# Expert attention at the boundary between rows: another order of the X-bank fills and of what reads them

## The reference

```python
sx = einsum('bsh,ndh->bnsd', layernorm(x), hl_w) + hl_b          # per head
q = einsum('bnsd,neod->bneso', sx, wq); k = sx @ wk; v = sx @ wv
att = softmax(einsum('bnesd,bntd->bnest', q, k) * d ** 0.5 + causal)
out = where(sx == 0, 0, einsum('bnest,bntd->bnesd', att, v))     # per head and expert
gs = softmax(out @ gate_w + gate_b)                              # over experts
hn = layernorm(sum_e out_e * gs_e + resid)                       # -> z, zn
hx = layernorm(mlp(hn) + hn)                                     # fc1, relu, fc2, each masked
return hx * softmax(hx @ fgate_w)                                # per head
```

## Time and profile before

| | |
|---|---|
| median of three runs | 2044.35 us |
| the profiled execution | 2043.27 us |
| its span | 2041.3 us |
| expert attention | some 570 to 1420 us of the span |
| busy TensorE, VectorE, ScalarE, GpSimd | 84%, 66%, 38%, 30% of the span |

### The profile page before, as it was taken

One profiled execution on the slowest core, in us unless ns is written; L12 is line 12 of the kernel. 1 busy time (PEld: TensorE's weight loads), 2 busy tenths in 40 slices (PEclk: granted clock), 3 DMA queues, 4 the chain that ended last, 5 costly groups with the idle time before them and its releaser, 6 DMA issues. The chain is left out here.

```text
span 2041.3 us, 45282 instructions
## 1 busy us (share of the span) xinstructions
PE 1713.3 (84%) x15237; PEld 1253.0 (61%) x15240; DVE 1350.3 (66%) x4295; ACT 775.0 (38%) x2210; POOL 602.4 (30%) x906
## 2 busy tenths in 40 slices
PE   1499999999669988888888888872899999788887
PEld 1266666666535555555555555551788888677776
DVE  6276666666526666666666666664766666588887
ACT  2254445454234444444444444420222222343443
POOL 2522222222134333333333333333211112222221
PEclk9999999999789887777777777775555555688988
DMA  2000000000000000000000000000000000000000
GB/s 112 1 2 0 0 0 0 0 0 0 1 1 1 2 1 0 0 0 0 0 0 0 0 0 0 0 1 0 1 0 0 0 0 1 1 5 5 6 4 13
DMA packets 6979, 8.13 MB, mean 4 GB/s; under 512 B 6272, under 2 KB 6272, under 8 KB 6784
## 3 DMA queue, kind: packets, MB, share of 16 engines
q1 hardware_dynamic: 6912, 7.25, 1.0%
HBM read 5.71 MB, written 1.54 MB: 4 GB/s over the span
## 5 line engine op out<-in xcount | busy, mean ns | idle before, releaser
L962 POOL TENSOR_SCALAR_AFFINE_SELECT ex_pT<-ex_pT 128x512 f32<-128x512 f32 (+1 forms) x256 | 135.7, 554 | 315.0 <-ACT ex_pT L1176 272.9
L604 ACT ACTIVATE al_prob<-al_S,al_negmax 94x94 f32<-94x94 f32 (+1 forms) x512 | 146.2, 376 | 180.0 <-DVE al_negmax L731 180.0
L505 PE MATMUL al_S<-al_kpad,al_qT 128*94 128x376 f32 x384 | 166.4, 516 | 0.0
L682 POOL TENSOR_TENSOR al_kpad<-al_kT,al_quad_mask 128x1504 f32<-128x1504 f32 x32 | 86.2, 2694 | 186.2 <-ACTq L619 186.2
L731 DVE TENSOR_REDUCE al_negmax<-al_S 94x2 f32<-94x376 f32 (+1 forms) x192 | 99.2, 542 | 62.6 <-PE al_S L506 56.7
L1599 POOL TENSOR_TENSOR ta_kk<-ta_ext 94x320 f32<-94x320 f32 x64 | 60.4, 962 | 246.2 <-DVE ta_qkn L1779 161.6
L1250 DVE TENSOR_REDUCE ex_negmaxA<-ex_R 128x4 bf16<-128x512 f32 x128 | 89.1, 696 | 56.9 <-PE ex_R L1028 51.4
L971 POOL TENSOR_TENSOR ex_zrstd<-ex_zvar,neg_half 94x16 f32<-94x16 f32 x34 | 98.6, 2900 | 28.9 <-DVE ex_zvar L1329 28.9
L741 DVE RECIPROCAL al_rec<-al_O 128x188 f32<-128x188 f32 x64 | 84.9, 1327 | 32.1 <-PE al_O L543 32.1
L1169 ACT ACTIVATE ex_pT<-ex_T 128x496 f32<-128x496 f32 x128 | 74.8, 584 | 76.0 <-PE ex_T L1066 76.0
L1176 ACT ACTIVATE ex_pT<-ex_T 128x496 f32<-128x496 f32 x128 | 74.8, 584 | 73.8 <-PE ex_T L1045 73.7
(11 more groups left out here) (321 smaller groups left out, 4413.3 us busy)
## 6 DMA issues: line engine op xcount, KB each, us to landing
tok_xin<-x_t SPq DMA_DIRECT2D x4, 760.0 KB, 7.3
wsb<-weights SPq DMA_DIRECT2D x1, 2531.0 KB, 14.0
out<-stream SPq DMA_DIRECT2D x16, 94.0 KB
tok_par<-tok_w SPq DMA_DIRECT2D x1, 4.5 KB, 1.7
```

Of the source, the lines that this page charges most:

```text
L505: nc.tensor.matmul(S[0:P, k, 0:2 * N], q, s, start=True, stop=False)
L604: last = nc.scalar.activation(p[:, k, cols], S[0:P, k, cols], ACT.Exp, bias=negmax[g % 2][:, m:m + 1])
L682: nc.gpsimd.tensor_tensor(kpad[par][:].rearrange("p j g n -> p j (g n)"), kT[:].rearrange("p g n -> p (g n)").unsqueeze(1).broadcast_to([1 ...
L962: nc.gpsimd.affine_select(out=view, in_=view, compare_op=ALU.is_ge, fill=0.0, base=shift, pattern=[[0, NH], [1, cols]], channel_multiplier ...
```

## The change

The order in which the X bank is filled and read around the boundary between turns changes, on all four engines.

- The ring becomes znT, fg, sx, pickA, kb01, kb23, q01, pickB, fc1, k, q23, v, xT, fc2. The xT fill moves from the first quarter of the next turn to the last quarter of the turn that normalises the row (behind max_scores), so xT of row t is made in turn t. In the first quarter znT goes ahead of `queries`, and fg ahead of `max_scores`. pickB goes ahead of `queries` in e = 2, q23 ahead of them in e = 3, and v ahead of max_scores.
- ScalarE copies qm ahead of the exponential of heads 0 and 1. In e = 1 and 3 the copies of kb01 and v stand between the two. tA_used is now signalled by that exponential itself; tA_exp is gone. fexp moves to e = 1, gate_exp and xT to the third slot of e = 3.
- GpSimd does rstd, zrstd and mixing at the head of quarters 1, 2 and 3, ahead of that quarter's causal pair. For zrstd and the mixing this is one pair earlier; rstd keeps its place.
- VectorE's list becomes: z reduces, hx mask | final gate logits (own tile ftop) | z adds | maxima(ru,2), mask(rt,3) | statistics, moments | zmean | pick A | maxima(ru,3), mask(ru,0) | zvar | xn | pick B | maxima(rf,0), mask(ru,1) | gate logits | h1m | zn | maxima(rf,1) | gate weights gs | mask(ru,2) | fout | hx add, which now reads fc2 of the same turn (row rm) at its end.

The diff, mostly its added lines:

```diff
@@ -879,10 +880,10 @@
-        FILLS = [("xT", FRONT), ("znT", MLP), ("fg", LAST), ("sx", FRONT),
+        FILLS = [("znT", MLP), ("fg", LAST), ("sx", FRONT),
...
-                 ("q23", FRONT), ("v", FRONT), ("fc2", MLP)]
+                 ("q23", FRONT), ("v", FRONT), ("xT", LN), ("fc2", MLP)]
...
...
@@ -1053,7 +1054,7 @@
-                    pe.wait_ge(sem["tA_used"], u + 1)
+                    need(pe, sem["tA_used"], u)
...
...
@@ -978,6 +968,17 @@
+                    r = t - UNIT
+                    if valid(r):
+                        p = pT[e % 2]
+                        pool.wait_ge(sem["tB_used"], r * NE + e + 1)
+                        pool.wait_ge(sem["tA_used"], r * NE + e + 1)
+                        pool.sem_inc(sem["settled"], 1)
+                        for first, cols, shift in ((0, K0, 0), (N, K1, QB)):
+                            view = p[:, :, first:first + cols]
+                            nc.gpsimd.affine_select(out=view, in_=view, compare_op=ALU.is_ge, fill=0.0, base=shift,
+                                                    pattern=[[0, NH], [1, cols]], channel_multiplier=-1)\
+                                .then_inc(sem["causal_done"], 1)
...
...
@@ -1097,39 +1098,39 @@
+                    if e == 1 and valid(rt):
+                        pe.wait_ge(sem["o_used"], NE * (rt + 1))
+                        fill(t, "pickA", picks(odd, slice(0, P)))
...
+                    if valid(nr):
+                        queries(nr, npar, ne).then_inc(sem["tA_full"], 1)
+                    if e == 0 and valid(rl):
+                        fill(t, "fg", by_halves(P, NH, lambda h: znT[odd][:, h * P:(h + 1) * P], lambda h: w("fgate")))
+                    if e == 1 and valid(rf):
+                        pe.wait_ge(sem["sx_used"], 2 * (rf + 1))
+                        fill(t, "kb01", padded_keys((0, 1)))
+                    if e == 3 and valid(rf):
+                        fill(t, "v", [(X[:, 0:C], sxT[odd][:, 0:K0], w("ewv")),
+                                      (X[:, C:2 * C], sxT[odd][:, QB:NP], w("ewv"))])
+
...
+                    if e == 3 and valid(t):
+                        pe.wait_ge(sem["xn_ready"], t + 1)
+                        fill(t, "xT", by_halves(C, P, lambda h: xn[:, h, :], lambda h: ident[0:P, 0:P]))
...
...
@@ -1167,32 +1168,32 @@
+                    if e == 1 and valid(rl):
+                        act.wait_ge(sem["fgate_ready"], rl + 1)
+                        nc.scalar.activation(fexp[:], fgate[:], ACT.Exp).then_inc(sem["fexp_ready"], 1)
+                    if e == 3 and valid(rf):
+                        act.wait_ge(sem["q23_full"], rf + 1)
+                        used("q23_used", qTb[odd][:, 2:4, 0:N], ALL, slice(0, 2 * N))
+
+                    if valid(nr):
+                        act.wait_ge(sem["tA_full"], nr * NE + ne + 1)
+                        nc.scalar.activation(qm[ne % 2][:], T[:, 0, QCOL:QCOL + N], ACT.Copy).then_inc(sem["m_used"], 1)
...
+                        act.wait_ge(sem["v_full"], rf + 1)
+                        for s, rows in enumerate((ALL, slice(QB, 128))):
+                            nc.scalar.activation(vals[odd][rows, s, :, 0:D],
+                                                 X[rows, s * C:(s + 1) * C].rearrange("p (n d) -> p n d", n=NH), ACT.Copy)\
+                                .then_inc(sem["v_used"], 1)
+                    if valid(ru):
+                        if not valid(nr):
+                            act.wait_ge(sem["tA_full"], u + 2)
+                        nc.scalar.activation(pT[e % 2][:, 0:2, :], T[:, 0:2, 0:PAIR], ACT.Exp).then_inc(sem["tA_used"], 1)
...
...
@@ -1200,12 +1201,12 @@
+                    if e == 3 and valid(rt):
+                        act.wait_ge(sem["gate_ready"], rt + 1)
+                        nc.scalar.activation(gate_exp[:], gate[:], ACT.Exp).then_inc(sem["gexp_ready"], 1)
+                    if e == 3 and valid(t):
+                        act.wait_ge(sem["xT_full"], t + 1)
+                        used("xT_used", xT[:], slice(0, C), slice(0, N))
...
...
@@ -1218,12 +1219,6 @@
...
@@ -1273,10 +1268,6 @@
...
@@ -1284,6 +1275,14 @@
+                if valid(rl):
+                    dve.wait_ge(sem["fg_full"], rl + 1)
+                    gates = X[0:P, 0:HALVES * NH].rearrange("p (h n) -> p h n", h=HALVES)
+                    link(red(ftop[:], gates, AX.X, ALU.max))
+                    tt(fgate[:], gates, ftop[:].unsqueeze(2).broadcast_to([P, HALVES, NH]), ALU.subtract)\
+                        .then_inc(sem["fgate_ready"], 1)
+                    dve.wait_ge(sem["fgate_ready"], rl + 1)
+                    dve.sem_inc(sem["fg_used"], 1)
...
...
@@ -1294,14 +1293,6 @@
...
@@ -1313,13 +1304,13 @@
+                if valid(rt):
+                    pick_heads(rt, 0, "pickA")
...
...
@@ -1328,8 +1319,20 @@
+                if valid(t):
+                    dve.wait_ge(sem["rstd_ready"], t + 1)
+                    need(dve, sem["xT_full"], t)
+                    for h in range(HALVES):
+                        last = ts(xn[:, h, :], stream[:, t * HALVES + h, :], moments[:, h, 0:1], rstd[:, h:h + 1],
+                                  ALU.subtract, ALU.mult)
+                    last.then_inc(sem["xn_ready"], 1)
...
+                if valid(rf):
+                    maxima(rf, 0)
+                if valid(ru):
+                    mask_values(ru, 1, par)
+                if valid(rt):
...
...
@@ -1338,21 +1341,10 @@
...
@@ -1360,6 +1352,17 @@
+                if valid(rf):
+                    maxima(rf, 1)
+                if valid(rt):
+                    dve.wait_ge(sem["gexp_ready"], rt + 1)
+                    flat = gate_exp[:].rearrange("p h n e -> p (h n) e")
+                    link(red(top[:], flat, AX.X, ALU.add))
+                    link(nc.vector.reciprocal(top[:], top[:]))
+                    tt(gate[:].rearrange("p h n e -> p (h n) e"), flat,
+                       top[:].unsqueeze(2).broadcast_to([P, HALVES * NH, NE]), ALU.mult).then_inc(sem["gs_ready"], 1)
+                if valid(ru):
+                    mask_values(ru, 2, par)
...
...
@@ -1368,17 +1371,10 @@
+                if valid(rm):
+                    dve.wait_ge(sem["fc2_full"], rm + 1)
+                    tt(hx[:], X[0:P, 0:HALVES * C].rearrange("p (h c) -> p h c", h=HALVES), over_halves("fc2_b"), ALU.add)\
+                        .then_inc(sem["fc2_used"], 1)
...
```

More of the change, by code:

```diff
@@ L831, in expert_attention @@
         top = sb("top", [P, HALVES * NH])
+        ftop = sb("ftop", [P, HALVES])
         gate_exp = sb("gate_exp", [P, HALVES, NH, NE])
@@ L953, in body @@
                 for e in range(NE):
[L954 to L964, removed]
                     r = t - LN
-                    if e == 0 and valid(r):
+                    if e == 1 and valid(r):
                         rstds(r)
@@ L1099, in body @@
                         scores(ru, par, e, (2, 3)).then_inc(sem["tB_full"], 1)
[L1100 to L1108, removed]
                     if e == 0 and valid2(rm):
@@ L1112, in body @@
                                                  lambda h: ident[0:P, 0:P]))
-                    if e == 1 and valid(rf):
-                        pe.wait_ge(sem["sx_used"], 2 * (rf + 1))
-                        fill(t, "kb01", padded_keys((0, 1)))
+                    if e == 1 and valid(rt):
+                        pe.wait_ge(sem["o_used"], NE * (rt + 1))
+                        fill(t, "pickA", picks(odd, slice(0, P)))
                     if e == 2 and valid(rt):
@@ L1119, in body @@
                         fill(t, "q23", projections((2, 3)))
+                    if valid(nr):
[8 more added lines that the diff above has]
+                                      (X[:, C:2 * C], sxT[odd][:, QB:NP], w("ewv"))])
                     if valid(fr):
                         max_scores(fr, fpar, fe)
-                    if e == 0 and valid(rl):
-                        fill(t, "fg", by_halves(P, NH, lambda h: znT[odd][:, h * P:(h + 1) * P], lambda h: w("fgate")))
                     if e == 1 and valid(rf):
@@ L1169, in body @@
                         nc.scalar.activation(pT[e % 2][:, 2:4, :], T[:, 2:4, 0:PAIR], ACT.Exp).then_inc(sem["tB_used"], 1)
[L1170 to L1186, removed]
                     if e == 0 and valid2(rm):
@@ L1220, in body @@
                         used("k_used", kT[odd][:, 0:N], ALL, slice(0, N), ACT.Identity, bias=one_row[:], scale=D ** 0.5)
[L1221 to L1226, removed]
             act.wait_ge(sem["consts"], CONSTS)
@@ L1274, in body @@
                 odd = 1 - par
[L1276 to L1279, removed]
                 if valid(rz):
@@ L1296, in body @@
                     mask_values(rt, 3, odd)
[L1297 to L1304, removed]
                 if valid(t):
@@ L1315, in body @@
                     last.then_inc(sem["stats_ready"], 1)
-                if valid(rt):
-                    pick_heads(rt, 0, "pickA")
                 if valid2(rz):
```

(15 more changed lines are left out.)

7 lines of the change are left out of this document (1 added, 6 removed).

## The result

The changed kernel takes 2019.71 us (median of 4 runs, 2016.77 to 2022.82) against 2044.31 us of the kernel before: a ratio of 0.988, 95% interval 0.986 to 0.990, 24.6 us less. The forecast was 1979 us. The time lies in the range (1940 to 2035) and on the side that was named, but the gain is 0.38 of the one forecast. It stands nearest to rival (b), in which the clock falls in every turn: 2029.

The account below looks back on a forecast made before the run. TensorE, nearly always busy, was held by a clock halving at turn boundaries: 22 turns from 25.59 to 22.8 us save 61 us, three earlier turns 4, giving 1979 us; own range 1960 to 2000, 8-in-10 range 1940 to 2035.

Parts of the forecast that it names:

- rival (b): Expert attention: clock falls in every turn as now, but the turn shortens to 24.9 us; total 2029 us; chance 0.17.
- The turn at the high level, 21.5 us: Expert attention: one turn without a clock fall, summed along VectorE and TensorE to 20.95 us, with corrections 21.5.
- A fall was priced at 3.4 us: Per turn: 10.1 us at the low level lose 4.4 us, less the 1.0 us kb01 wait absorbed.
- I take 4 turns in 10: Share of turns in which the clock falls, bounds 0 and 10; gives a mean turn of 22.8 us.
- the three early ones: Three turns ahead of the 22: 24.0 us each falling to 22.8, a gain of 4 us.
- the undecided size: Boundary between rows: about 1 us of TensorE idleness may or may not lower the clock; less should keep it high.
- hx ends 1.72 after scores(0) starts: Turn boundary: mask, fout and hx on VectorE end 1.72 us after scores(0) starts, so TensorE waits 1.0 us.
- the z adds: First quarter, VectorE: adds meeting GpSimd's causal pair every turn cost 0.4 us; by the skill's rule the turn is 22.1.
- kb01 waits 1.0: First pick: zmean stands ahead of pick_heads, so kb01 waits about 1.0 us, where it had 0.18.
- rival (c): Slower: the new kb01 wait prolongs the low stretch to 17 us, turn 27.0 us, total 2075 us; chance 0.15.
- GpSimd covered: GpSimd's new order costs nothing: third causal pair covered by 3 us, the mix ahead of the fourth also covered.
- xn costs nothing: Reading xn a turn ahead costs nothing: rstd is ready some 5 us before, and xn fills idle time before pickB.

Follow-up runs that it names:

- x2: Changed kernel with six extra unused matmuls on TensorE between scores(0) and the znT fill, in the wait for hx: 1968.6 us, ratio 0.965.
- x7: Kernel before with one part of the change alone: VectorE reads the final gate logits ahead of maxima(ru, 2). 2019.7 us, ratio 0.988.
- x10: Kernel before with two VectorE changes alone: final gate logits read ahead of maxima(ru, 2), hx added at the turn's end ahead of fout. 1969.8 us, ratio 0.965.
- x3: Changed kernel with VectorE's gate weights gs moved behind fout, so that GpSimd's mixing starts after fout: 2004.1 us, ratio 0.982.
- x11: x1 with four extra unused matmuls on TensorE ahead of the pickA fill, in the wait for ScalarE's copy of sx: 1909.4 us, ratio 0.935.
- x1: Changed kernel with VectorE's hx add moved ahead of fout: 1944.7 us, ratio 0.952.
- x8: Changed kernel with GpSimd's old order: zrstd and the mixing behind their quarter's causal pair. 2045.0 us, ratio 1.001.
- x9: Changed kernel with the xT fill back in the next turn's first quarter, ahead of znT: 2054.4 us, ratio 1.0055.
- x4: Kernel before with four extra unused matmuls on TensorE between scores(0) and the xT fill, in the wait for hx: 1982.7 us, ratio 0.970.

## Why the prediction was wrong

**What held.** The clock is what the turn turns on; sx no longer waits for the gate logits; VectorE's wait for the mixing is gone. The turn at the high level, 21.5 us, was 21.8 in x2 with its extra matmuls, but in part by luck: there kb01 waits 0.42 us where the sum has 1.0, and pickA 1.09 where it has nothing. A fall was priced at 3.4 us; in x2 a turn with 10.2 us at the low level lasts 25.7, 3.9 more than one without. The changed kernel itself has no turn without a fall among the 22, so its 24.72 against the 24.9 of rival (b) does not test the price by itself.

**The step that failed: "I take 4 turns in 10".** The clock falls in all of them, 22 of 22. With 1.0 in place of 0.4 the same sum gives 24.9 us a turn, 15 us less over 22 turns and 3 more over the three early ones: 2032, against 2019.7 measured. So this term is the miss of 41 us and more. Of the 12 us left, 4 are the turn (24.72) and 5 the early turns, which lasted 69.9 us where they had lasted 72.1; 3 are not placed, and the start of the block varies by more.

Three things are in the term. I called about 1 us the undecided size from one wait of 1.07 us that was survived; x7, with 0.93 in each turn, has a low stretch in every one, and that single row was the exception. The wait is not 1.0 but 1.74 us. And I read only every other fall. The level in the earlier trace rows falls at 1014.6, when the wait for hx had just begun: scores end at 1014.55, and the row that waited starts a microsecond later.

```profile
1015.51 0.89 PE L992 MATMUL ex_X<-ident,ex_xn 94*64 94x94 f32 x4 [0.96 <-DVE ex_hx L1278]
```

This wait can't have made the level fall. So it is with 11 of the 22 falls of the kernel before; the other 11 come some 0.65 us after the end of their wait (1.02 us, then 0.50 from 786.0). A size of the boundary wait at which the level is undecided, on which the 0.4 rests, can't be read from these rows. x10's fall without a boundary wait says the same.

**"hx ends 1.72 after scores(0) starts".** In the profiled turn above it is 2.38 (scores start at 993.96, hx ends at 996.34). The rest of the turn has fout with 2.3 us from its first step to hx where I took 1.54: I moved GpSimd's mixing earlier and counted what it freed, but did not look at what VectorE does at its new time. The rule of the Trainium skill (SBUF — State Buffer, "Who interferes with whom") that the prediction applied to the z adds applied here as well. The trace agrees with it: the 8-column product stands until a multiply of GpSimd is through, 0.75 us against 0.16, fout stands beside the causal pair, 0.68 against 0.29, and x3, where neither runs beside them, gives both lengths back.

**"kb01 waits 1.0".** 0.19 in the changed kernel, since TensorE is at the low level there, as the argument against rival (c) had it; 0.42 and 0.61 in x2 and x11, where it is not. Above all pickA, ahead of it, waits 1.1 to 1.4 us in x1 and x2, a wait that my sum did not have: I had followed the X bank's ring, but not the buffer sxT, which the copy of sx must wait for.

**"GpSimd covered", "xn costs nothing".** As costs these were right; what I missed is that the parts carry one another. hx as the last of VectorE's list puts all of its second half on the boundary, so GpSimd's order there is worth 25 us (x8; it moves zrstd and the mixing together, and the trace has the wait at zrstd), and xT ahead of it 35 us (x9). That they pay back what the late hx takes, and no more, is argued from x7, which is as fast without any of them.

**Open.** The difference of 0.87 us a turn is not divided further. TensorE's listed waits hardly changed, 2.5 to 2.3 us a turn, so it lies in the 0.9 us less of low level and in the work that left the low stretch, as argued and not shown. What makes the level fall is open too. That TensorE's waits matter is shown: where hx comes earlier (x1, x10) or matmuls stand in the wait (x2, x4, x11), the low level shrinks. But the idle time does not sort the kernels: over the 22 turns x7 has TensorE idle least of all, 1.94 us a turn, with 11.2 us at the low level, and x2 has 2.45 with 2.0. A rival, that the level follows how much work the matmuls around the boundary are and not how long TensorE stands, fits x2, x4 and x11 as well and was not tried alone; for that one would add the same matmuls where TensorE does not wait. Why a fall follows 0.93 us in x7 and not 1.07 at 735.91 was not tried either.

## What to carry to other kernels

Where TensorE's clock falls and rises within one turn of a loop, a wait costs more than its length: here the one wait for hx was 1.7 us long and its removal gave 2.6 us a turn, although a new wait of 1.4 came up elsewhere. Before a wait is held to cause a fall, set the start of each fall beside it: in the kernel before, half of them came too early. Ask of every moved read what stands ahead of it on its own engine, and put the read that frees a shared bank ahead of all that nobody waits for. Before reordering four engines, try each early read alone.

## What was not expected of the hardware

Matmuls of no use made the kernel faster: six of them a turn 51 us (x2), four 60 us (x4), four on top of x1 35 us (x11). In x10 the level fell with no wait at the boundary, and in x2 it stayed high through a wait of 1.09 us in 13 turns of 22. And a VectorE product of 94 x 8 elements took 0.75 us instead of 0.16 beside a GpSimd multiply of 94 x 256.
